# Attention scores from four 32-row strips of TensorE instead of two of 64, with the k/v product, k's bias and the turn of x2 moved in the step

## The reference

```python
def rms_norm(x, g): return x * rsqrt(mean(x * x, axis=-1, keepdims=True) + 1e-6) * g
def attention(q, k, v):                       # 16 heads of 16
    p = softmax(einsum('bqhd,bkhd->bhqk', q, k) / sqrt(16)); return einsum('bhqk,bkhd->bqhd', p, v)
def xattn(x, context, ...):                   # the context has 64 tokens, all of them "image" tokens
    q = rms_norm(x @ w_q.T + b_q, g_q)
    k = rms_norm(context @ w_k_img.T + b_k_img, g_k_img)
    v = context @ w_v_img.T + b_v_img
    return attention(q, k, v) @ w_o.T + b_o
def moe(x, ...):                              # 32 experts, 4 chosen per token, and a shared expert
    scores = softmax(x @ gate_w.T); tw, ti = top_k(scores, 4); tw = tw / tw.sum()
    g = silu(x @ Rg.T @ Ug[e].T @ Cg[e].T); u = x @ Ru.T @ Uu[e].T @ Cu[e].T
    y = sum over chosen e of tw[e] * ((g * u) @ Rd.T @ Ud[e].T @ Cd[e].T)
    return y + shared(x)
x = x + xattn(layernorm(x), ctx_2048, ...)
return x + moe(layernorm(x), ...)
```

## Time and profile before

| | us |
|---|---|
| median of 3 runs (their range) | 837.47 (835.49 to 838.66) |
| the profiled execution: its time | 836.83 |
| the profiled execution: its span | 835.1 |
| PE busy in the span | 765.4 (92%) |
| DVE busy | 583.5 (70%) |
| ACT busy | 470.4 (56%) |
| POOL busy | 490.7 (59%) |
| mean granted TensorE clock | 0.979 |

### The profile page before, as it was taken

The page is one execution under the profiler, slowest core; times in us unless marked ns, Lnnn a source line. Parts: engine busy times, 40 slices in busy tenths (PEclk is TensorE's granted clock), DMA queues, the critical chain, the costliest instruction groups (busy, mean ns, idle before and its releaser), DMA issues.

```text
span 835.1 us, 22131 instructions
## 1 busy us (share of the span) xinstructions
PE 765.4 (92%) x6030; PEld 637.6 (76%) x6031; DVE 583.5 (70%) x2018; ACT 470.4 (56%) x1410; POOL 490.7 (59%) x700
## 2 busy tenths in 40 slices
PE   4899999999999999745999999999999999999996
PEld 2566666666666666525989998999899989889996
DVE  2578888888888888753656665666566656388787
ACT  2678888888888888723444444444344444233332
POOL 1125666666666666666555555555555555587776
PEclk9999999999999999967999999999999999999998
DMA  7345756555555555658544444344444445598881
GB/s 200 103 127 168 220 178 180 180 178 176 180 178 176 176 176 163 198 196 286 158 131 122 126 132 129 123 127 131 126 125 127 131 121 164 180 334 276 285 273 45
DMA packets 101890, 142.02 MB, mean 170 GB/s; under 512 B 16171, under 2 KB 83043, under 8 KB 101219
## 3 DMA queue, kind: packets, MB, share of 16 engines
q1 hardware_dynamic: 83235, 96.99, 39.2%
q0 software_dynamic: 14592, 40.99, 13.9%
q10 hardware_dynamic: 4032, 3.67, 1.3%
HBM read 86.73 MB, written 58.82 MB: 174 GB/s over the span
## 4 chain that ended last, share of the span: by engine, by line
PE 85%; DMA 4%; issue 3%; DVE 3%; SPq 1%; ACT 1%; POOL 1%; POOLq 0%; DVEq 0%; ACTq 0%
PE bank L1245 9%; PE bank L1253 9%; PE bank L472 6%; PE bank L1267 6%; PE bank L1269 6%; PE bank L1278 4%; PE bank L1260 4%; PE bank L529 4%; PE bank L419 4%; PE bank L436 4%; PE bank L505 4%; PE bank L547 3%; PE bank L458 3%; PE bank L1316 3%; PE bank L1296 2%
## 5 line engine op out<-in xcount | busy, mean ns | idle before, releaser
L1378 POOL DMA_INDIRECT yt_d<-yo,name_i x160 | 157.8, 986 | 29.4 <-issue 19.9
L771 POOL DMA_INDIRECT xs_d<-rgu,sloti x128 | 128.5, 1004 | 39.5 <-issue 32.5
L1422 DVE TENSOR_TENSOR h<-bank,gated 128x176 f32<-128x176 f32 x160 | 54.7, 342 | 86.5 <-ACT gated L1331 86.0
L1245 PE MATMUL bank<-down_w,rdt 128*128 x320 | 97.6, 387 | 18.5 <-issue 17.4
L1253 PEld LDWEIGHTS bank<-ht,rd_w 88*128 88x128 f32 x640 | 96.6, 191 | 8.4 <-issue 0.4
L1327 ACT ACTIVATE rdt<-bank 128x128 f32<-128x128 f32 x160 | 44.4, 278 | 103.2 <-PE bank L1253 103.1
L1331 ACT ACTIVATE gated<-bank 128x176 f32<-128x176 f32 x160 | 50.8, 318 | 86.6 <-PE bank L1269 86.6
L1253 PE MATMUL bank<-ht,rd_w 88*128 88x128 f32 x640 | 97.6, 274 | 0.0
L1376 POOL TENSOR_TENSOR fence<-ones 128x1 f32<-128x1 f32 x160 | 29.6, 185 | 112.0 <-DVE name_i L1412 111.6
L1411 DVE COPY yo<-bank 128x256 f32<-128x256 f32 x160 | 67.3, 421 | 24.8 <-PE bank L1245 24.6
L1417 DVE COPY ht<-bank 88x256 f32<-88x256 f32 x160 | 67.3, 420 | 21.5 <-PE bank L1260 12.3
(11 more groups left out here) (163 smaller groups left out, 1906.8 us busy)
## 6 DMA issues: line engine op xcount, KB each, us to landing
xg<-xs_d SPq DMA_DIRECT2D x160, 128.5 KB, 2.1
got<-yt_d SPq DMA_DIRECT2D x32, 512.0 KB, 5.3
raw<-in_raw SPq DMA_DIRECT2D x32, 496.0 KB
v<-v SPq DMA_DIRECT2D x128, 34.0 KB, 2.0
xs_d<-in_spare SPq DMA_DIRECT2D x4, 1028.0 KB, 6.3
xin<-in_x SPq DMA_DIRECT2D x32, 128.0 KB
ctxt<-in_ctxt SPq DMA_DIRECT2D x32, 128.0 KB
xres<-in_x SPq DMA_DIRECT2D x32, 128.0 KB
```

The costliest lines, as they stand in the source:

```text
L771: nc.gpsimd.indirect_dma_start(xs_d, bass.IndirectOffsetOnAxis(sloti[:, b, k:k + 1], 0), rgu[:, b, k, :], None)\
L1245: nc.tensor.matmul(y_ps[b], rdt[:, b, :], weight(down_w, DOWN), start=True, stop=True)\
L1378: nc.gpsimd.indirect_dma_start(yt_d, bass.IndirectOffsetOnAxis(name_i[:, b, :], 0), yo[:, b, :], None)\
```

## The change

GROUPS and GH become 4 and 2: a strip has 32 features and 2 heads. There are 16 score matmuls of 32 rows, 64 columns and 128 streamed columns, in four banks, and ktm has two copies instead of four. The scores take the lower halves of banks 0 to 3; k, v, the turned q and the turned k take the upper halves, one bank each, so kv_in has four matmuls of 256 streamed columns for two of 512. On PE kv_in moves from in front of the scores to behind x_turn, and x2_turn from in front of the scores to behind them. qk_turn waits for `soft` of the step before; scores_ready waits for k's bias and v's copy, since these read the same banks. On ACT the copy of v (v17) moves from behind the squares to behind xn1t. On DVE k's bias moves into the step before, between gate_weights and norm2, and mean_square moves behind o_norm. PE's wait for the output bias in step 3 moves behind qk_turn.

```diff
-GROUPS, GH = 2, 4
+GROUPS, GH = 4, 2
+STRIP = P // GROUPS
-            s_ps = bank03[:, 0:GROUPS, :]
-            kv_ps = bank03[:, 2, :]
-            qkt_ps = bank03[:, 3, :].rearrange("p (c t) -> p c t", c=2 * CH)
+            s_ps = bank03[:, 0:GROUPS, 0:DIM]
+            k_ps = bank03[:, 0, DIM:2 * DIM]
+            v_ps = bank03[:, 1, DIM:2 * DIM]
+            qt_ps = bank03[:, 2, DIM:2 * DIM].rearrange("p (c t) -> p c t", c=CH)
+            kt_ps = bank03[:, 3, DIM:2 * DIM].rearrange("p (c t) -> p c t", c=CH)
@@ kv_in
-                    if past(i, 1):
-                        pe.wait_ge(kb_done, i)
-                        pe.wait_ge(v_done, i)
+                    if past(i, 2):
+                        pe.wait_ge(ssub_done, i - 1)
-                    for c in range(CH):
-                        m = nc.tensor.matmul(kv_ps, ctxt[:, b, c, :], wkv[:, c, :], start=(c == 0), stop=(c == CH - 1))
+                    for part, k in ((k_ps, 0), (v_ps, DIM)):
+                        for c in range(CH):
+                            m = nc.tensor.matmul(part, ctxt[:, b, c, :], wkv[:, c, k:k + DIM],
+                                                 start=(c == 0), stop=(c == CH - 1))
@@ qk_turn, ahead of its transposes
+                    if past(i, 1):
+                        pe.wait_ge(ssub_done, i)
@@ scores_ready
                     pe.wait_ge(ktm_done, i + 1)
-                    if past(i, 1):
-                        pe.wait_ge(ssub_done, i)
+                    if live(i + 1, TILES):
+                        pe.wait_ge(kb_done, i + 2)
+                        pe.wait_ge(v_done, i + 2)
@@ scores
-                                feats = slice(64 * g, 64 * (g + 1))
-                                m = nc.tensor.matmul(s_ps[SEQ * n:SEQ * (n + 1), g, c * 256:(c + 1) * 256],
+                                feats = slice(STRIP * g, STRIP * (g + 1))
+                                m = nc.tensor.matmul(s_ps[SEQ * n:SEQ * (n + 1), g, c * P:(c + 1) * P],
@@ PE's body
-                    if at_step(s, 3):
-                        pe.wait_ge(bo_done, 1)
-                        pe.wait_ge(halves_done, 2)
                     x_turn(s, ph)
+                    kv_in(s, ph)
                     down_product(s, ph)
                     qk_turn(s, ph)
+                    if at_step(s, 3):
+                        pe.wait_ge(bo_done, 1)
+                        pe.wait_ge(halves_done, 2)
                     p_turn(s, ph, 0)
 ...
                     p_turn(s, ph, 1)
-                    kv_in(s, ph)
                     scores_ready(s, ph)
+                    scores(s, ph)
                     x2_turn(s, ph)
-                    scores(s, ph)
@@ ACT's body, behind xn1t (and taken out behind the squares of k)
+                        act.wait_ge(kv_psum, i + 1)
+                        if past(i, 2):
+                            act.wait_ge(v2_in[b], landed(i, 2, b, 64) - 64)
+                        nc.scalar.activation(
+                            v17[:, b, :, :, 0:HD],
+                            v_ps.rearrange("p (r g d) -> p r g d", r=2, g=PAIRS),
+                            ACT.Copy).then_inc(v_done, 1)
@@ k_bias
-                    i, b = s - 1, (ph - 1) % 2
+                    i, b = s, ph % 2
@@ DVE's body
-                    k_bias(s, ph)
                     soft_max(s, ph)
+                    o_norm(s, ph)
                     mean_square(s, ph)
-                    o_norm(s, ph)
 ...
                     gate_weights(s, ph)
+                    k_bias(s, ph)
                     norm2(s, ph)
```

More of the change, by code:

```diff
@@ L432, in p_times_v @@
                     for blk in range(PAIRS):
-                        group, c, hp = blk // 4, blk // 2 % 2, blk % 2
-                        pair = PAIRS // CH * c + GH // 2 * group + hp
+                        group, c = blk // CH, blk % CH
+                        pair = PAIRS // CH * c + group
                         for n in range(2):
@@ L480, in qk_turn @@
                     pe.wait_ge(kn_done, i + 1)
+                    if past(i, 1):
+                        pe.wait_ge(ssub_done, i)
                     for c in range(CH):
-                        nc.tensor.transpose(qkt_ps[:, c, :], qb[:, b, c * P:(c + 1) * P], ident[:, :])
+                        nc.tensor.transpose(qt_ps[:, c, :], qb[:, b, c * P:(c + 1) * P], ident[:, :])
                     for c in range(CH):
-                        m = nc.tensor.transpose(qkt_ps[:, CH + c, :], kb[:, b, c * P:(c + 1) * P], ident[:, :])
+                        m = nc.tensor.transpose(kt_ps[:, c, :], kb[:, b, c * P:(c + 1) * P], ident[:, :])
                     m.then_inc(qkt_psum, 1)
@@ L659, in body @@
                         for c in range(CH):
-                            nc.scalar.activation(qt[:, b, c, :], qkt_ps[:, c, :], ACT.Copy,
+                            nc.scalar.activation(qt[:, b, c, :], qt_ps[:, c, :], ACT.Copy,
                                                  scale=gqk[:, c:c + 1])
@@ L664, in body @@
                     if live(i, TILES):
-                        kt = qkt_ps[:, CH:2 * CH, :].rearrange("p c (n k) -> p (c n) k", n=2)
+                        kt = kt_ps.rearrange("p c (n k) -> p (c n) k", n=2)
                         for g in range(GH):
@@ L690, in body @@
                                              accum_out=ssq[:, b, 1:2]).then_inc(ssq_done, 1)
[L691 to L696, removed]
                     i, b = s - 5, (ph - 5) % 2
@@ L860, in soft_max @@
                     dve.wait_ge(s_psum, i + 1)
-                    sv = s_ps.rearrange("p g (h k) -> p (g h) k", k=SEQ)
-                    mv = smax[:, b, :, :].rearrange("p g h -> p (g h)")
-                    nc.vector.tensor_reduce(mv, sv, AX.X, ALU.max).then_inc(smax_done, 1)
+                    nc.vector.tensor_reduce(smax[:, b, :, :], s_ps.rearrange("p g (h k) -> p g h k", k=SEQ),
+                                            AX.X, ALU.max).then_inc(smax_done, 1)
                 def soft(s, ph):
@@ L868, in soft @@
                         return
-                    sv = s_ps.rearrange("p g (h k) -> p (g h) k", k=SEQ)
-                    mv = smax[:, b, :, :].rearrange("p g h -> p (g h)")
                     dve.wait_ge(smax_done, i + 1)
                     nc.vector.tensor_tensor(
-                        prob[:, b, :, :].rearrange("p q (r k) -> p (q r) k", r=2), sv,
-                        mv.unsqueeze(2).broadcast_to([P, HEADS, SEQ]), ALU.subtract).then_inc(ssub_done, 1)
+                        prob[:, b, :, :].rearrange("p (g c) (r k) -> p g (c r) k", c=CH, r=2),
+                        s_ps.rearrange("p g (h k) -> p g h k", k=SEQ),
+                        smax[:, b, :, :].unsqueeze(3).broadcast_to([P, GROUPS, CH * GH, SEQ]),
+                        ALU.subtract).then_inc(ssub_done, 1)
                 def q_bias(s, ph):
@@ L883, in k_bias @@
                 def k_bias(s, ph):
-                    i, b = s - 1, (ph - 1) % 2
+                    i, b = s, ph % 2
                     if not live(i, TILES):
                         return
-                    if at_step(s, 1):
+                    if at_step(s, 0):
                         dve.wait_ge(ld_next, 16 * len(loads_next))
                     dve.wait_ge(kv_psum, i + 1)
-                    nc.vector.tensor_tensor(kb[:, b, :], kv_ps[:, 0:DIM], bk[:, :], ALU.add).then_inc(kb_done, 1)
+                    nc.vector.tensor_tensor(kb[:, b, :], k_ps, bk[:, :], ALU.add).then_inc(kb_done, 1)
                 def o_norm(s, ph):
```

## The result

The changed kernel takes 844.93 us (median of 5 runs, 843.59 to 846.82) against 837.47 (median of 5, 835.49 to 841.94): the ratio is 1.0086, 95% interval 1.0062 to 1.0110. It is slower by 7 us, 0.9%. The profiled execution took 843.59 us, 6.8 more than that of before.

The account below looks back on a forecast made before the run. The prediction took PE's chain to bound the kernel, with ACT's way through x2_turn to ot setting the changed step: +3.9 us over 28 steps, -2 at the start, -1 at the end, so 838 us, range 828 to 847.

Parts of the forecast that it names:

- rival B: Scores on PE don't get shorter than 1.02 us; step 10.65 us, time 844; chance 0.13.
- rival C: POOL's and DVE's round takes over, slower with k_bias and mean_square inside: step 10.68 us, time 843.5; chance 0.12.
- The scores: Score matmuls on PE: 0.6 us instead of 1.02, with eight array parts working side by side.
- ktm: ACT's copies, two fewer: -0.72 us; complete at E + 1.79, scores start about E + 1.86 (E: end of qk_turn).
- x2_turn waits for down_w: PE waits about 0.25 us ahead of x2_turn for ACT's down_w copy; x2_turn starts 2.71 us after qk_turn's end.
- ACT from xn2t to ot: ACT's work between these two: 3.01 us instead of 3.44, without a gap.
- project waits for ot: PE waits about 0.4 us for ACT's ot; project can start 6.62 us after qk_turn's end.
- from project to qk_turn's end: PE's stretch from project's start, with kv_in now inside it: 3.86 us.
- the step: Distance between two x_turns on PE: 10.48 us against 10.34, +3.9 us over 28 steps.
- DVE and POOL: k_bias hides in DVE's idle time; mean_square's move makes POOL's round about 10.27 us, still under the step.
- rival A: PE's saving comes through: step 9.92 us, time 822, or 828 if POOL's 10.12 us is the floor; chance 0.22.
- Start and end: Outside the 28 counted steps: -2 us in the first steps, -1 us in step 33.

Follow-up runs that it names:

- e2: Changed kernel with ACT's down_w copy in front of the second half of probt: 835.70 us.
- e3: Changed kernel with ACT's copies of the rows to be scattered moved from in front of ot to behind the exponentials of the scores: 839.28 us.
- e6: Changed kernel with x2_turn back in front of the scores on PE: 860.49 us.
- e7: Changed kernel with mean_square back in front of o_norm on DVE: 845.91 us.
- e8: e4's kernel with DVE's norm2 and slot_rows of a step moved behind norm1_stats of the next: 829.47 us.
- e4: Changed kernel with both ACT edits, e2's early down_w copy and e3's late row copies: 835.47 us.
- e1: Kernel before with x2_turn moved behind the scores, plus a one-column matmul that carries the scores' wait: 863.84 us.
- e10: e8's kernel with down_product on PE moved from behind kv_in to in front of the scores: 830.36 us.
- e9: Changed kernel with two strips of 64 rows instead of four of 32, four ktm copies and the one-column matmul: 881.81 us.
- e11: e8's kernel with two strips of 64 rows instead of four of 32, four ktm copies and the one-column matmul: 872.34 us.
- e5: Kernel before with only the one-column matmul ahead of the scores, as control for e1: 843.80 us.

## Why the prediction was right or wrong

The forecast was 838 (828 to 847), no change; the time is 844.93. It lies in that range, but outside the forecast's own range of 834 to 843 (steps of 10.38 to 10.62 us), and "slower" had 0.33 where no change had 0.40. By the number alone rivals B (844) and C (843.5) did better than the forecast. What speaks for the forecast is the mechanism: PE waits for down_w and for ot in every step, and e2, e3 and e6 move the time through these two waits. Its size was too small.

- *The scores*: 0.59 us by the sum and 0.6 taken, 0.62 measured (e6's rows). Right; rival B is out.
- *kv_in*: 1.72 us predicted, 221.16 - 219.43 = 1.73 measured. Right.
- *ktm*: two copies and the start of probt behind them took 213.43 - 212.56 = 0.87 us, not 0.72. A pair is not half of the four's 1.43. The scores' weight load waited 0.31 us for ktm in each step and they started at E + 1.93, not 1.86; the wait for down_w covers that.
- *x2_turn waits for down_w*: right. x2_turn's matmuls started 0.28 us late in 19 of 19 steps, where 0.25 was predicted. With E = 211.16 + 0.38 = 211.54, x2_turn started at E + 2.91 instead of 2.71 and xn2t at E + 3.44 instead of 3.18. ktm is 0.15 of the 0.20, and the way from down_w's end to x2_turn another 0.09 (0.14 us where 0.05 was taken).
- *ACT from xn2t to ot*: right, without a gap; 2.85 us instead of 3.01, a miss in the other direction.
- *project waits for ot*: right, 0.31 us at E + 6.71 where 6.62 was predicted.
- *from project to qk_turn's end*: this term was mis-sized. 222.19 - 218.25 = 3.94 us instead of 3.86. I had taken project's start from the chain of waits, which counts a piece from the end of the one before it; matmuls overlap, and in PE's own order of time project started 0.15 us earlier (214.78 for 214.93).
- *the step*: 6.71 + 3.94 = 10.65 in this step, 10.68 on average, 10.48 predicted. 0.20 us too little in each of 28 steps is 5.6 us, and that is the miss.
- *DVE and POOL*: right in the result for the changed kernel. k_bias ran in the idle time in front of norm2, and e7 shows the round is not the bound. The argument had a flaw: "POOL's round" of 10.12 us is the distance of one repeated instruction, and that is the step. In the kernel before it alternates between about 10.12 and 10.42, in the changed one between 10.22 and 11.06, with over 2 us of waiting for DVE inside each time. So the 10.12 was no floor for rival A and no start for rival C's sum. e8 shows that DVE's order comes to bear once ACT's is mended.
- *Start and end*: -2.1 at the start (-2 predicted) and -0.3 at the end (-1 predicted); how the parts named for them share in this was not measured.
- *Rival A* failed by the argument made against it, ACT's way; with that way mended the kernel comes down to 835.5 (e4), and near A's 828 only with DVE's order mended too (e8, 829.5).

What I had not seen is in e1: I priced x2_turn's move in the old order at 0.3 to 0.4 us, as if project had had 0.6 us of slack behind ot. It had none, and the move cost 11.25 - 10.49 = 0.76.

Not settled: what sets the step of e8 and e10, and why e6, e9 and e11 lost 5 us more behind step 32 than the kernels they are compared with (e9 4 us ahead of step 4 as well). No run has the 32-row strips in the old order, so what they would bring there, where PE has no wait to hide them in, is open. Nor was the one-column matmul run inside the changed order, so its share of e9 and e11 is an estimate.

## What to carry to other kernels

When a piece of work is moved on the engine that bounds a pipeline, ask what it was covering: here the scores stood between x2_turn and project, and their 1.02 us hid the other engine's whole way from the one to the other. After such a move, follow the second engine's strict order from each thing that it releases to the next (down_w, xn2t, ot), and count what it does in between that nobody waits for: swapping two neighbouring copies was worth 9 us, more than the change had cost. An engine that has become less busy can still be the one that is late. A wait in the list isn't yet a cost: in e1 and e7 PE waited half a microsecond for DVE in every step and would have waited for ACT otherwise. And the time from one instruction of an engine to its next turn is the step on any engine; which one sets it, only an edit to its work can tell.

## What the runs showed of the hardware

Float32 matmuls on 32x64 parts of the array overlap too, though less fully than those on 64x64 parts: 32 records of 128 columns take 0.62 us (e6) where one after the other they would take 3.44, 5.5 at once on average out of eight; 16 records of 256 columns take 1.02 us, 3.4 at once out of four.

Two ktm copies on ACT take 0.87 us from their start to the next instruction's, and four take 1.43: the second pair adds only 0.56.

A single 128x128 float32 matmul with one streamed column cost 0.14 us of the step between x2_turn and the scores (e5) and took 0.31 us behind a wait (e9), more than its one column. Whether that is its weight load or the change between kinds of matmul was not tested.
